# Cross attention on one Trainium2 core: the context keys' product moved behind the pair's other value products, and a wider transposition of the context probabilities

## The chip, the cores and the metric

The kernel runs on one core of a Trainium2 chip. The metric is the device time of one execution in microseconds (us). Three executions of the kernel before took 1844.14, 1845.26 and 1848.06 us; the median is 1845.26. One more execution was profiled. Engines are named as in the profile: PE is the matrix engine (PEld its weight loads), DVE the vector engine, ACT the scalar engine, POOL the general engine, SP the one that issues most DMAs.

## The reference, cut to what matters

The program is a two-layer decoder: four batches of 512 tokens with 128 features, and a context of 32 tokens per batch. Six blocks follow one another, each with a residual and a layer norm. The change is in the second block of layer 0, an attention over the 512 tokens and the 32 context tokens together:

```python
x = layer_norm(image_embeds, ln1_g, ln1_b)   # the 32 context tokens
l = layer_norm(latents, ln2_g, ln2_b)        # the 512 tokens
q = l @ Wq                                    # 16 heads of 64
kv = jnp.concatenate([x, l], axis=1) @ Wkv    # 544 keys and values
w = jnp.einsum('bhqd,bhkd->bhqk', q * scale, k * scale)
w = jax.nn.softmax(w, axis=-1)
out = jnp.einsum('bhqk,bhkd->bhqd', w, v)
return out.transpose(0, 2, 1, 3).reshape(B, S_lat, INNER) @ Wo
```

The third block, the next attention (16 heads of 8), begins inside the end of this one.

## The kernel before, in words

Everything is float32 here. Heads are taken in pairs: a *pair of heads* g (32 of them: four batches times eight) fills both halves of the array's 128 columns or rows. Each pair of heads has four *steps*, one for each 128 queries, so the stage is a loop of 128 steps i, which each engine's program walks through in its own order (`b2_pe`, `b2_act`, `b2_dve`; seven more rounds on PE and DVE drain it). The position of a step in its group of four is r = i % 4. There is no scheduler: the order is as the code writes it, and engines meet by semaphores.

In round i:

- PE computes the **scores** of step i (`scores`, L639: four matmuls of 64 rows, two at a time on the two row halves, into banks 0 to 3 of PSUM). They wait until ACT has done both exponentials of step i-1, since there is one set of banks.
- DVE takes two maxima (`neg_max`, L826), ACT two exponentials (L777), DVE then divides by the sums one round later (`normalise`, L832 and L834).
- PE **transposes** the probabilities of step i-2 (`transposes`, L653: eight of 128x128 for the 512 tokens' keys; L658: one for the 64 columns with both heads' context keys, into the rows 0 to 63 of bank 6). ACT copies the eight out (L785); DVE copies bank 6 out once for the four steps of a pair of heads (`ctx_read`, L857).
- PE multiplies the transposed probabilities with the values (`pv`, L675). This product of a pair of heads has five parts k, each with one matmul for each head, the two side by side in column halves: k = 0 to 3 are the 512 tokens (128 rows, 64 columns each), k = 4 is the context (32 rows, 64 columns each). All five add up in bank 7. Parts 0 and 1 stand at r = 3, parts 2 and 3 at r = 0, part 4 at r = 1, right behind the scores. So part 4 of the pair of heads g is in round i = 4g + 9.
- The sum is read out of bank 7 by DVE (`pv_read`, L851) in the same round, behind the two maxima of step i in DVE's order.

Bank 7 is shared. Besides the sum of the five parts it takes the projections of the next queries and keys (L596), of the next values (L628), matmuls of the norms (L623, L612), and the output projection (L684). Each of these waits for the semaphore `bank7_read`, that is for the reader of the use before. At r = 1 the use of bank 7 stands behind the transpositions, and the reading it waits for is `pv_read`.

A record of a matmul in the profile is one of two passes: a float32 matmul has two (x8 for four matmuls), a float32 transposition one.

The head of the third block runs inside the last rounds: its scores are L1112, their maxima L1390, on POOL L1337 to L1345 split its queries and keys, SP writes the rows of ones (L1520) and packs them by DMA.

Of the kernel before, what the change touches and what calls it, by code (L numbers as in the profile page):

```python
# [21 lines left out]
B, T, D = 4, 512, 128  # L22
H, HD = 16, 8
XH, XD = 16, 64
S = 32
# [49 lines left out]
def program(nc, xT, ctxT, vecs, groups, out, stages=6):  # L75
    ctx = ExitStack()
    with ctx:
# [5 lines left out]
        def sem(name):  # L83
            if name not in sem_of:
                sem_of[name] = ctx.enter_context(nc.semaphore(name))
            return sem_of[name]
# [26 lines left out]
        ps = ctx.enter_context(nc.psum_tensor("ps", [128, 8, 512], F32))  # L113
# [185 lines left out]
        P = TAPS // 2  # L299
# [146 lines left out]
        if stages >= 2:  # L446
            Wq, Wkv, Wo = wt["Wq"], wt["Wkv"], wt["Wo"]
            XP, XPAIRS, XHALF = B * 8, B * 32, KEYS // 2
# [3 lines left out]
            x_prob = c(6 * KEYS).rearrange("p (s k) -> p s k", s=3)  # L452
# [15 lines left out]
            def prob_of(P, r):  # L468
                return x_prob[:, P % 3, KEYS * r:KEYS * r + KEYS]
# [43 lines left out]
            for i in range(XPAIRS + 7):  # L513
                r, n = i % 4, i // 4 + 1
# [70 lines left out]
            def b2_pe(e):  # L585
                def free7(use):
                    if at7[use] > 1:
                        e.wait_ge(sem("bank7_read"), at7[use] - 1)
# [36 lines left out]
                def v_proj(b, j, bank):  # L625
                    k, a = divmod(j, 2)
                    e.wait_ge(*latents(b))
                    e.matmul(ps[:, bank, :], x_aux[:, b, k * 128:k * 128 + 128], Wkv[:, 1024 + a * 512:1536 + a * 512],  # L628
                             start=True, stop=True).then_inc(sem("v_proj"), 1)
# [14 lines left out]
                def transposes(P):  # L644
                    n, q = divmod(P, 4)
                    if P == 0:
                        e.wait_ge(sem("v_read"), 8)
                    for r in range(2):
                        e.wait_ge(sem("prob_done"), 2 * P + r + 1)
                        if P:  # L650
                            e.wait_ge(sem("evacuated"), 2 * P + r - 1)
                        for k in range(4):
                            i = e.transpose(ps[:, 4 + r, k * 128:k * 128 + 128], prob_of(P, r)[:, MAIN[r] + k * 128:MAIN[r] + k * 128 + 128],  # L653
                                            ident)
                        i.then_inc(sem("transposed"), 1)
                    if q == 0 and n:
                        e.wait_ge(sem("ctx_probs"), n)
                    e.transpose(ps[0:2 * S, 6, q * 128:q * 128 + 128], x_prob[:, P % 3, T:T + 2 * S],  # L658
                                ident).then_inc(sem("ctx_turned"), 1)

                def pv(g, parts):
                    b, hp = divmod(g, 8)
                    if parts[0] == 0:
                        e.wait_ge(sem("evacuated"), 8 * (g + 1))
                        if b == 0:
                            e.wait_ge(sem("v_read"), 8)
                        free7(("pv", g))
                    for k in parts:
                        if k == 4:
                            e.wait_ge(sem("ctx_probs"), g + 1)  # L670
                        for j in range(2):
                            h = 2 * hp + j
                            v_of = x_vv[:, b % 2, k, :] if k < 4 else x_vc[S * j:S * j + S, b, :]
                            p_of = x_pt[:, 2 * g % 4 + j, k, :] if k < 4 else x_ptc[S * j:S * j + S, g % 2, :]
                            i = e.matmul(ps[64 * j:64 * j + 64, 7, :], v_of[:, h * 64:h * 64 + 64], p_of,  # L675
                                         start=(k == 0), stop=(k == 4), skip_group_check=True)
                    if parts[-1] == 4:
                        i.then_inc(sem("pv_done"), 1)
# [13 lines left out]
                for i in range(XPAIRS + 7):  # L692
                    r, n = i % 4, i // 4 + 1
                    if i < XPAIRS:
                        scores(i)
                    if i < 2:
                        for j in range(4 * i, 4 * i + 4):
                            if j >= 3:
                                e.wait_ge(sem("v_read"), j - 2)
                            v_proj(0, j, 4 + j % 3)  # L700
                    if r == 1:
                        if 0 <= (i - 9) // 4 < XP:
                            pv((i - 9) // 4, (4,))
                    if i == XPAIRS + 5:
                        head_pe(e, range(*HEAD[i]))
                    if i == XPAIRS + 6:
                        head_pe(e, range(HEAD[i][0], HEAD[i][0] + 3))
                    if r == 2:
                        if out_at(i - 1) is not None:
                            out(out_at(i - 1), 1)  # L710
                        elif n < XP:
                            proj("q", n)
                    if r == 3:
                        if v_at(i):
                            free7(("v",) + v_at(i))
                            v_proj(*v_at(i), 7)
                        elif early_at(i):
                            early(early_at(i))
                        elif chain_at(i):
                            chain(chain_at(i))  # L720
                        if late(i) and n < XP:
                            proj("k", n)
                    if 0 <= i - 2 < XPAIRS:
                        transposes(i - 2)
                    if r == 3 and 0 <= (i - 7) // 4 < XP:
                        pv((i - 7) // 4, (0, 1))
                    if r == 0 and 0 <= (i - 8) // 4 < XP:
                        pv((i - 8) // 4, (2, 3))
                    if r == 1:
                        if out_at(i) is not None:  # L730
                            out(out_at(i), 0)
                        elif v_at(i):
                            free7(("v",) + v_at(i))
                            v_proj(*v_at(i), 7)
                        elif early_at(i):
                            early(early_at(i))
                        elif chain_at(i):
                            chain(chain_at(i))
                    if r == 2 and n < XP:
                        proj("q" if late(i) else "k", n)  # L740
                    if i in HEAD_QK:
                        head_qk_pe(e, HEAD_QK[i])
                    if i in HEAD and i != XPAIRS + 5:
                        head_pe(e, range(HEAD[i][0] + (3 if i == XPAIRS + 6 else 0), HEAD[i][1]))
# [229 lines left out]
        def narrow(nth, src, src_ready, dst, tag, load, wq, wk, wv, wo, bias_v=None, rope=None, early=None, head=0, border=None):  # L974
# [82 lines left out]
            for step in range(STEPS):  # L1057
                G, u = step // 16, step % 16
                g, r = raw_group(step)
# [436 lines left out]
            def sp(e):  # L1496
                for b in range(B):
                    for i, ready in ((0, 1), (1, 3), (2, 4)):
                        for w in range(2):
                            e.wait_ge((split_q, split_k)[w], 4 * b + ready)  # L1500
                            for r in ((i, i + 3) if w and i < 2 else (i,)):
                                e.dma_start(scr[b, w, 8 * r:8 * r + 8].rearrange("d (h t) -> (d h) t", h=H),
                                            (parts if b else parts_0)[:, w, i, :]).then_inc(parts_out, 16)
                    e.wait_ge(parts_out, 16 * 8 * (b + 1))
                    if early is not None and b < 2:
                        e.wait_ge(sem("pv_done"), (24, XP)[b])
                    for hg in range(4):
                        if b:
                            e.wait_ge(packed[hg], 16 * 6 * (batches_0 + b))
                        if b >= 2:  # L1510
                            e.wait_ge(score2, 64 * (b - 2) + 16 * (hg + 1))
                        for w in range(2):
                            pack(e, b, w, hg)
                    if b == 0:
                        e.wait_ge(ones_set, nth + 1)
                        for a in range(2):
                            if a and early is not None:
                                e.wait_ge(sem("pv_done"), XP)
                            for hg in range(4):
                                e.dma_start(k_pack[a][hg][ROWS:ROWS + 3, :, :],  # L1520
                                            ones_row.unsqueeze(1).to_broadcast([3, 4, T])).then_inc(ones_rows, 16)
# [1399 lines left out]
```

## Time and profile before

| | us |
|---|---|
| median of three executions | 1845.26 |
| the profiled execution | 1845.25 |
| its span, first to last instruction | 1843.4 |
| PE busy in the span | 1653.6 (90%) |
| DVE busy | 1271.4 (69%) |
| ACT busy | 949.4 (52%) |
| scores of step 0 to the last context product | about 60 to 674 |

The profiled execution lies at the median. The span leaves 1.85 us around it. Times in the rows are us from the span's start. The clock that was granted to PE is given as a share of full speed (2.4 GHz). Share of busy time says little about what a change is worth: PE's share in the stage in question is high, and what has to be read is which wait ends last before each piece.

### The profile page before, as it was taken

Reading aid. Unit: us, or ns where it says so; the run is one execution under the profiler, and the core shown is the slowest. Engines: PE = TensorE matmul, PEld = TensorE weight load, DVE = VectorE, ACT = ScalarE, POOL = GpSimd, SP = SyncE. Lnnn points to the kernel's source line nnn. Section 1 sums busy time; section 2 is a strip of 40 time slices with the busy share of each in tenths; the row PEclk is TensorE's granted clock in tenths of the full one; section 3 lists DMA queues with packets and bytes.
Section 4 is the critical chain, followed back from the end, with each engine's and each line's share of the span. In section 5 each row is a group of like instructions: output and inputs, shape, how many; then the busy total and the mean of one; then the engine's idle time right before and its main releaser. Section 6 shows DMA issues by size and latency. Waiting matters only on the chain.

```text
span 1843.4 us, 24921 instructions
## 1 busy us (share of the span) xinstructions
PE 1653.6 (90%) x8074; PEld 736.0 (40%) x8074; DVE 1271.4 (69%) x2994; ACT 949.4 (52%) x2053; POOL 304.5 (17%) x465
## 2 busy tenths in 40 slices
PE   7899999999999989999899988444798899999998
PEld 3355455545544432222244331222443355444443
DVE  7576666767667768888565578999666677762423
ACT  3565556556645516666633566333236366664333
POOL 1000000000001021121277200000000222114443
PEclk9999999999999989999999999777799799999999
DMA  4000000000000220240000000000100512100000
GB/s 193 1 1 1 1 1 1 1 1 1 1 1 21 55 59 23 73 116 2 1 0 1 0 1 1 1 1 1 69 1 1 147 55 73 32 2 1 1 0 23
DMA packets 19806, 44.36 MB, mean 24 GB/s; under 512 B 3872, under 2 KB 13024, under 8 KB 18912
## 3 DMA queue, kind: packets, MB, share of 16 engines
q1 hardware_dynamic: 19200, 42.39, 7.6%
q8 instruction: 66, 1.08, 0.2%
q14 instruction: 60, 0.49, 0.1%
q10 hardware_dynamic: 480, 0.39, 0.1%
HBM read 32.74 MB, written 9.44 MB: 23 GB/s over the span
## 4 chain that ended last, share of the span: by engine, by line
PE 75%; DVE 16%; ACT 5%; issue 3%; POOL 1%; DMA 0%; ACTq 0%; POOLq 0%; SPq 0%; DVEq 0%
PE ps L675 8%; PE ps L639 8%; PE ps L653 6%; PE ps L1226 6%; PE ps L1264 5%; PE ps L1112 5%; PE ps L1699 3%; PE ps L1700 3%; PE ps L596 3%; PE ps L1596 3%; PE ps L1612 3%; PE ps L1707 3%; DVE arena L2063 2%; PE ps L684 2%; DVE arena L2050 2%
## 5 line engine op out<-in xcount | busy, mean ns | idle before, releaser
L1390 DVE TENSOR_REDUCE stat<-ps 128x1 f32<-128x512 f32 (+3 forms) x512 | 279.1, 581 | 86.6 <-PE ps L1116 43.0
L1321 ACT ACTIVATE arena<-ps 128x512 f32<-128x512 f32 (+3 forms) x512 | 247.1, 515 | 154.3 <-PE ps L1264 83.3
L826 DVE TENSOR_REDUCE stat<-ps 128x1 f32<-128x544 f32 x256 | 173.4, 719 | 163.0 <-PE ps L639 163.0
L777 ACT ACTIVATE arena<-ps,stat 128x544 f32<-128x544 f32 x256 | 180.7, 711 | 201.9 <-DVE stat L826 201.9
L1264 PE MATMUL ps<-arena 75*128 75x512 bf16 (+1 forms) x480 | 163.1, 344 | 11.7 <-ACT arena L1321 9.5
L1112 PE MATMUL ps<-arena 72*128 72x128 bf16 (+1 forms) x480 | 163.0, 348 | 8.0 <-DVE stat L1390 7.8
L675 PE MATMUL ps<-arena 128*64 128x512 f32 (+1 forms) x640 | 159.2, 609 | 4.7 <-DVE arena L845 3.3
L639 PE MATMUL ps<-arena 64*128 64x272 f32 x1024 | 152.1, 415 | 5.1 <-ACT arena L777 4.3
L785 ACT COPY arena<-ps 128x512 f32<-128x512 f32 x256 | 137.3, 594 | 15.5 <-PE ps L653 15.5
L653 PEld LDWEIGHTS ps<-wA_sb,arena 128*128 128x128 f32 x1024 | 115.1, 142 | 70.1 <-issue 68.9
L653 PE MATMUL ps<-wA_sb,arena 128*128 128x128 f32 x1024 | 138.3, 278 | 0.0
L639 PEld LDWEIGHTS ps<-arena 64*128 64x128 f32 x1024 | 88.2, 186 | 113.0 <-ACT arena L777 67.6
L1730 DVE TENSOR_TENSOR arena<-arena,ps 128x512 f32<-128x512 f32 (+1 forms) x76 | 52.2, 687 | 116.6 <-ACT arena L1719 116.5
L834 DVE TENSOR_SCALAR arena<-arena,stat 128x544 f32<-128x544 f32 x256 | 120.1, 511 | 4.5
L1949 ACT ACTIVATE reg<-arena,reg 128x16 f32<-128x16 f32 x254 | 66.3, 315 | 103.3 <-DVE arena L2063 103.3
L1226 PE MATMUL ps<-arena 128*32 128x512 f32 (+3 forms) x1024 | 116.2, 527 | 0.0
L958 POOL COPY arena<-arena 64x32 f32<-64x32 f32 x64 | 15.4, 240 | 582.1 <-PE ps L639 548.2
L1719 ACT ACTIVATE arena<-ps 128x512 f32<-128x512 f32 (+1 forms) x76 | 45.3, 597 | 127.5 <-PE ps L1700 127.5
L2163 PE MATMUL ps<-reg 128*128 128x512 f32 (+1 forms) x120 | 66.7, 674 | 41.0 <-DVE reg L2095 33.2
L1744 POOL TENSOR_TENSOR arena<-arena 128x512 f32<-128x512 f32 x64 | 82.7, 1292 | 95.4 <-DVE arena L1730 95.4
L1112 PEld LDWEIGHTS ps<-arena 72*128 72x128 bf16 x480 | 47.3, 99 | 116.8 <-DVE stat L1390 65.1
L1632 POOL TENSOR_TENSOR reg<-reg,arena 128x512 f32<-128x512 f32 x64 | 88.7, 1404 | 24.5 <-ACT reg L1622 23.6
(391 smaller groups left out, 2775.2 us busy)
## 6 DMA issues: line engine op xcount, KB each, us to landing
arena<-b_parts SPq DMA_DIRECT2D x180, 96.0 KB
b_parts<-arena SPq DMA_DIRECT2D x64, 128.0 KB, 1.9
reg<-wM_dram SPq DMA_DIRECT2D x1, 3072.0 KB, 10.0
reg<-wB_dram SPq DMA_DIRECT2D x1, 2048.0 KB, 12.4
reg<-wM_dram SPq DMA_DIRECT2D x1, 2048.0 KB, 16.7
reg<-wD_dram SPq DMA_DIRECT2D x1, 1817.0 KB, 10.7
wF_sb<-wF_dram SPq DMA_DIRECT2D x1, 1476.0 KB, 19.8
reg<-b_parts SPq DMA_DIRECT2D x12, 96.0 KB
```

Source lines behind the costliest of these rows:

```text
L639: i = e.matmul(ps[:, 2 * r + a, 0:XHALF], x_qq[64 * r:64 * r + 64, n % 2, q * 128:q * 128 + 128], x_kt[64 * r:64 * r + 64, n % 2, S * (1 - ...
L653: i = e.transpose(ps[:, 4 + r, k * 128:k * 128 + 128], prob_of(P, r)[:, MAIN[r] + k * 128:MAIN[r] + k * 128 + 128], ident)
L675: i = e.matmul(ps[64 * j:64 * j + 64, 7, :], v_of[:, h * 64:h * 64 + 64], p_of, start=(k == 0), stop=(k == 4), skip_group_check=True)
L777: e.activation(prob_of(P, r).rearrange("p (a k) -> p a k", a=2), score_banks(r), ACT.Exp, bias=x_neg[:, at_:at_ + 1], accum_out=x_sums[:, ...
L785: e.copy(x_pt[:, 2 * n % 4 + r, :, q * 128:q * 128 + 128], ps[:, 4 + r, :].rearrange("p (k q) -> p k q", k=4)).then_inc(sem("evacuated"), 1)
L826: e.tensor_reduce(x_neg[:, n % 4:n % 4 + 1], score_banks(r), AX.XY, ALU.max, negate=True).then_inc(sem("max_done"), 1)
L834: e.tensor_scalar(prob_of(P, r), prob_of(P, r), x_inv[:, at_ + r:at_ + r + 1], None, ALU.mult).then_inc(sem("prob_done"), 1)
L1112: i = e.matmul(ps[:, step % S1, 0:keys(u)], q_pack[pack][hg][0:ROWS, h, q * 128:q * 128 + 128], k_pack[pack][hg][0:ROWS, h, 0:keys(u)], st ...
L1226: i = e.matmul(ps[32 * j:32 * j + 32, 5, q0:T], vv[:, b % 2, p, G % 4 * 4 + j, :], p_t[:, n_ % 2 * 4 + j, q0:T], start=(p == 0), stop=(p = ...
L1264: i = e.matmul(ps[:, S1 + m % S2, q0:T], k_pack[pack][hg][0:ROWS + 3, h, k * 128:k * 128 + 128], q_pack[pack][hg][0:ROWS + 3, h, q0:T], st ...
L1321: e.activation(p_t[:, m % 8, q0:T], ps[:, S1 + m % S2, q0:T], ACT.Exp).then_inc(exp_done, 1)
L1390: e.tensor_reduce(nm[:, G % 2, u // 4, u % 4:u % 4 + 1], ps[:, step % S1, 0:keys(u)], AX.X, ALU.max, negate=True).then_inc(max_done, 1)
```

## The change

Three edits. The context product (part 4) moves from r = 1, behind the scores, to r = 0, behind parts 2 and 3. The transposition of the context probabilities takes 128 columns (the 64 context columns and 64 more that nobody reads) in place of 64. And SP waits for the split of the second batch before it writes the second set of rows of ones.

```diff
@@ transposes
-                    e.transpose(ps[0:2 * S, 6, q * 128:q * 128 + 128], x_prob[:, P % 3, T:T + 2 * S],
+                    e.transpose(ps[:, 6, q * 128:q * 128 + 128], x_prob[:, P % 3, T:T + 128],
                                 ident).then_inc(sem("ctx_turned"), 1)
@@ the loop of b2_pe
                             v_proj(0, j, 4 + j % 3)
-                    if r == 1:
-                        if 0 <= (i - 9) // 4 < XP:
-                            pv((i - 9) // 4, (4,))
                     if i == XPAIRS + 5:
...
                     if r == 0 and 0 <= (i - 8) // 4 < XP:
                         pv((i - 8) // 4, (2, 3))
+                        pv((i - 8) // 4, (4,))
@@ sp, the rows of ones
                             if a and early is not None:
                                 e.wait_ge(sem("pv_done"), XP)
+                                e.wait_ge(split_q, 8)
+                                e.wait_ge(split_k, 8)
```

PE's order from a transposition at r = 0 to the use of bank 7 at r = 1, before. L675 64x512 is the value product, L639 the scores, L653 and L658 the transpositions, L628 a projection of values:

```order
L658 MATMUL ps<-wA_sb,arena 64x128
L675 MATMUL ps<-arena 64x512 x4
L639 MATMUL ps<-arena 128x272 [waits ctx_keys,bank7_read,exp_done]
L639 MATMUL ps<-arena 128x272 x3
L675 MATMUL ps<-arena 64x512 [waits ctx_probs]
L675 MATMUL ps<-arena 64x512
L653 MATMUL ps<-wA_sb,arena 128x128 [waits evacuated,prob_done]
L658 MATMUL ps<-wA_sb,arena 64x128
L628 MATMUL ps<-reg,x_aux 128x512 [waits c_normed,bank7_read]
```

The same place after the change:

```order
L658 MATMUL ps<-wA_sb,arena 128x128
L675 MATMUL ps<-arena 64x512 x4
L675 MATMUL ps<-arena 64x512 [waits ctx_probs]
L675 MATMUL ps<-arena 64x512
L639 MATMUL ps<-arena 128x272 [waits ctx_keys,bank7_read,exp_done]
L639 MATMUL ps<-arena 128x272 x3
L653 MATMUL ps<-wA_sb,arena 128x128 [waits evacuated,prob_done]
L658 MATMUL ps<-wA_sb,arena 128x128
L628 MATMUL ps<-reg,x_aux 128x512 [waits c_normed,bank7_read]
```

The two matmuls of part 4 now stand ahead of the scores of r = 1. DVE's order at r = 1 after the change (the line numbers are two lower than before; L824 the maxima, L849 `pv_read`, L855 `ctx_read`):

```order
L824 TENSOR_REDUCE stat<-ps 128x1 [waits exp_done,scored] x2
L849 COPY cent<-ps 128x512 [waits pv_done]
L830 RECIPROCAL stat<-stat 128x2 [waits exp_done]
L832 TENSOR_SCALAR arena<-arena,stat 128x544 [waits dve_link]
L832 TENSOR_SCALAR arena<-arena,stat 128x544
L855 COPY arena<-ps 64x512 [waits pv_done,ctx_turned]
```

Nothing moved there: the reading of bank 7 still stands behind the two maxima, which wait for the scores of the same round.

## Rows read from the trace of the kernel before

**Rows 1.** The page, part 1: busy time, share and instructions of each engine.
```profile
PE 1653.6 (90%) x8074; PEld 736.0 (40%) x8074; DVE 1271.4 (69%) x2994; ACT 949.4 (52%) x2053; POOL 304.5 (17%) x465
```

**Rows 2.** Windows: stretch, length, busy time of PE, PEld, DVE, ACT, POOL, clock, DMA.
```profile
409.15:413.27 4.12, 4.12 (x27) 2.11 (x26) 2.34 (x5) 2.14 (x6) 0.00 (x0) 1.00 0.00 0
413.27:417.55 4.28, 4.28 (x25) 2.12 (x24) 3.03 (x7) 2.63 (x7) 0.00 (x0) 1.00 0.00 0
```

**Rows 3.** Chain that ended last, from 411 us: start, us, what.
```profile
411.47 1.87 PE ps L675 x8
413.34 1.12 PE ps L639 x8
414.46 1.00 PE ps L675 x4
415.46 1.02 PE ps L653 x8
416.49 0.11 PE ps L658
...
421.97 1.12 PE ps L639 x8
```

**Rows 4.** Timeline, 411 to 417 us: start, us, engine, line, op, [idle before <-releaser].
```profile
411.88 0.14 PEld L675 LDWEIGHTS ps<-arena 128*64 128x64 f32 x2 [0.29 <-issue]
...
412.31 0.14 PEld L675 LDWEIGHTS ps<-arena 128*64 128x64 f32 x2 [0.29 <-issue]
...
413.27 1.19 PE L639 MATMUL ps<-arena 64*128 64x272 f32 x8
...
414.49 1.36 DVE L826 TENSOR_REDUCE stat<-ps 128x1 f32<-128x544 f32 x2 [1.74 <-PE ps L639]
...
415.76 0.68 DVE L851 COPY cent<-ps 128x512 f32<-128x512 f32 x1
...
416.49 0.30 PEld L623 LDWEIGHTS ps<-reg,wA_sb 128*128 128x128 f32 x2 [0.17 <-DVE cent L851]
```

**Rows 5.** Line L851 (`pv_read`): who waited for it, us and times.
```profile
  PEld ps L628: 2.0, 12
  PEld ps L623: 1.4, 8
  PEld ps L612: 1.0, 6
  PEld ps L684: 0.5, 3
```

**Rows 6.** Timeline of the one r = 1 without a use of bank 7, from 501.20 us.
```profile
501.20 1.19 PE L639 MATMUL ps<-arena 64*128 64x272 f32 x8
...
504.73 1.19 PE L639 MATMUL ps<-arena 64*128 64x272 f32 x8 [0.21 <-ACT arena L777]
```

**Rows 7.** Timeline, 655 us: a context transposition, then the next block's scores.
```profile
655.20 0.27 PE L658 MATMUL ps<-wA_sb,arena 128*64 128x128 f32 x1
...
655.31 0.81 PE L1112 MATMUL ps<-arena 72*128 72x512 bf16 x3
```

**Rows 8.** Chain that ended last, 668 to 676 us: the end of the stage.
```profile
668.98 2.22 POOL arena L1345 x2
...
672.42 0.39 PE ps L1131 x4
672.81 1.03 PE ps L675 x4
673.86 0.69 DVE dev L851
```

**Rows 9.** Timeline, 652 to 674 us: DVE and SP at the end of the stage.
```profile
652.94 1.89 DVE L1390 TENSOR_REDUCE stat<-ps 128x1 f32<-128x512 f32 x3 [2.33 <-PE ps L1112]
...
670.15 3.08 DVE L1390 TENSOR_REDUCE stat<-ps 128x1 f32<-128x512 f32 x5 [2.01 <-PE ps L1112]
...
673.86 2.94 SPq L1520 DMA_DIRECT2D arena<-arena  x4
```

## The prediction

> **What bounds the kernel now.** I read part 1 of the page first: PE is busy 90% of the span, so every place where PE is the last to be ready costs time, and every place where it waits hides some [rows 1]. Then the windows of single rounds of the attention. A round at r = 0 lasts 4.12 us and one at r = 1 lasts 4.28 us, both at the full clock [rows 2]. From the starts of the scores (L639) I took the lengths of all rounds: they repeat to 0.01 us, so one place read closely stands for some thirty.
>
> The chain that ended last lies on PE alone at r = 0 and r = 1: parts 2 and 3 of the value product 1.87 us, scores 1.12, part 4 (L675 x4) 1.00, eight transpositions 1.02, the context transposition 0.11 [rows 3]. Read without the next view, this says that the order of these pieces is free, and only their sum counts. The timeline says otherwise. At r = 1 the scores start at 413.27. DVE is idle for 1.74 us, waiting for them, and takes both maxima from 414.49 on. Only behind these stands the reading of bank 7, at 415.76 for 0.68 us, to 416.44. PE's next use of bank 7 starts at 416.49, and its releaser is this reading [rows 4]. So the use starts 416.49 - 413.27 = 3.22 us behind the scores. PE itself comes to it after 1.12 + 1.00 + 1.02 + 0.11 = 3.25 us by the chain's lengths, or, by the recorded 0.17 us of idle time less the 0.11 us of L658, about 0.06 us before the reading is done. Two paths of equal length thus end there: PE's (scores, part 4, transpositions) and DVE's (scores, maxima, reading). DVE's does not hold part 4 unless part 4 ends later than the maxima, and it does not.
>
> How often: the reading's waiters are 12 + 8 + 6 + 3 = 29 uses of bank 7 [rows 5]. There are 30 rounds at r = 1 with a part 4 inside the 128 steps; the thirtieth has no use of bank 7.
>
> **The change part by part.**
>
> Part 4 at r = 0. It comes behind parts 2 and 3 and ahead of the scores of r = 1, which wait for nothing but PE's own end there (4.12 us a round against 3.53 us where the exponentials bound it [rows 2, 6]). So the round at r = 0 grows by all that part 4 costs. Its price in the old place is 1.00 us [rows 3]. It is two passes' time and a switch: the pairs of weight loads of parts 2 and 3 follow at 412.31 - 411.88 = 0.43 us, so two pairs stream for 0.86 us, and 0.14 us are left for what comes with a change of shape. The new place is bounded from both sides: 0.86 us if the step from 128 rows and 64 columns to 32 rows and 64 columns costs nothing, 1.00 us if it costs what the step out of 32 rows costs now. No row shows this step. The nearest is the step from the scores, 64 rows and 128 columns, to the transpositions, 128 rows and 128 columns: there too only the rows change, and the scores take 1.12 us as they do ahead of part 4, where rows and columns change (the piece at 421.97 against that at 413.34) [rows 3]. I take 1.00.
>
> The Trainium skill, "TensorEngine Tiling (Array Packing)", Key Properties, says "Mode switching requires drain", for a change of the tiling mode and not just of the tile. The trace agrees with it in the 1.12 us just named. By this rule the step costs its switch, and the sum stays at 1.00 a piece.
>
> Part 4 taken out of r = 1. PE then has scores 1.12 and transpositions 1.02 + 0.11 = 2.25 us, and reaches the use of bank 7 one microsecond sooner. DVE's path stays as it is, since its order has the reading behind the two maxima of that round and they wait for its scores. That bank 7 is complete a round earlier does not help: DVE stands in its queue at the first maximum, which is the 1.74 us of idle time [rows 4], and now stands there about 2.7 us. The use still starts 3.22 us behind the scores, with about 1.0 us of idle PE ahead of it. The round stays at 4.28 us, and nothing is taken back. Behind the waiting matmul in PE's queue stand the scores of r = 2, and the maxima and exponentials that wait for them.
>
> The thirtieth round at r = 1 has no such use. It lasts 504.73 - 501.20 = 3.53 us, and the scores that end it wait for ACT's exponential [rows 6]; scores, maxima and exponentials have the same lengths after. It stays too.
>
> So 30 rounds at r = 0 grow by 1.00 us: +30.0 us. Rounds at r = 2 and 3 have no edit but the transposition.
>
> The transposition at 128 columns. Its weight load grows from 64 to 128 columns, and lies beside the transposition before it. Its own step on PE is 0.11 us now, with the wide ones' eight at 1.02 less their 0.14 of entry, so 0.11 each [rows 3]: the step is set by the 128 moving columns, which stay. If the cover failed, a step of 0.11 would be added at each of 128 places, 14 us; the wide ones stand against it, since they step by 0.11 with that very load. A gain could come if the narrow one cost a switch: but after a narrow one the next block's 128-column scores follow at 655.31 - 655.20 = 0.11 us [rows 7], no switch at all. I take zero; the bounds are -0.09 and +0.11 for each, and the upper one is the less likely, since the same load is seen hidden eight times in each round.
>
> The Trainium skill, "TensorEngine Tiling (Array Packing)", Restrictions, says that column tiling disables the transpose mode for float32. By that the narrow transposition cannot have been column-tiled, and the wide one removes no switch; the trace agrees in the same 0.11 us.
>
> SP's new waits. The second rows of ones were issued at 673.86, released by the last part 4 [rows 9]. The split of the second batch ends at 668.98 + 2.22 = 671.20, ahead of it [rows 8]. After the change the last part 4 comes earlier against its surroundings and the split's end is what is late, but ahead of the old time. Queued behind on SP are the parts and packs of the second batch, which come no later than before. Cost zero. Without that cover, the wait would push four issues (2.94 us [rows 9]) and what is queued behind them back by as much as the split ends late.
>
> The end of the stage. The pair of heads 30 has part 4 at 653, between the next block's first three scores and transpositions. DVE had been idle 2.33 us waiting for those three [rows 9], and from there its maxima pace the chain. Part 4 now stands ahead of them: +1.00 us. The last pair has its part 4 at 672.81, behind the POOL chain's turn at 672.42, and DVE reads it at 673.86 [rows 8]. DVE's five maxima from 670.15 end at 673.23, so it idled 0.63 us for part 4. With part 4 ahead of the five, they start 1.00 later (DVE was idle for PE there, 2.01 us) and the 0.63 goes: +0.37 us.
>
> Sum: 30.0 + 1.0 + 0.4 = +31.4 us. All that follows hangs rigidly on the end of this stage. The profiled execution took 1845.25 us (span 1843.4, 1.85 around it), the median of the runs is 1845.26, so no correction: 1876.6 us.
>
> **The rivals.**
>
> No switch between parts 3 and 4. For it: both are 64 columns wide. Against it: the 1.12 us at 421.97. Each of 32 pieces is 0.14 shorter: 31.4 - 32 x 0.14 = +26.9, 1872.2 us.
>
> The wide transposition saves a drain behind it after all. For it: parts 2 and 3, which follow such a transposition, take 1.87 us where four pairs stream for 4 x 0.43 = 1.72, so 0.15 goes at their two ends [rows 3, 4]. Against it: the step of 0.11 in [rows 7], and the products are column halves, so a switch stays behind a full-width piece. At 0.09 in each of 128: 31.4 - 11.5 = +19.9, 1865.2 us.
>
> The clock falls. PE gets a new idle microsecond in 29 rounds. Against it: the windows at r = 0 and 1 have 1.00, as has the stretch with the exponential wait. If in each of 30 groups of four rounds 0.33 us of work ran at half speed, 30 x 0.33 = 10 us are added: 1886 us.
>
> The other side: it is not slower. The mechanism would be that the switch around part 4 is saved while the use of bank 7 does not wait for DVE at r = 1, because the reading is done in DVE's idle 1.74 us ahead of the maxima. Then PE goes on at 2.25 us. It decides as soon as the reading ends by 2.25 us behind the scores' start, and where the exponentials (3.53 us a round) are not next. PE would save the one switch between the scores and part 4, or pay none: 32 x -0.14 = -4.5, 1840.8 us. If the exponentials are next, r = 0 and 1 together are 5.12 + 3.53 = 8.65 against 8.40, +0.25 x 30 = +7.5, 1852.8 us. Against both: DVE's order is unchanged, and each of the 29 uses has DVE as its releaser now [rows 5].
>
> **How the numbers follow.** Forecast (1876.6, its own scatter 1874 to 1879) 0.68. No switch 0.17. A cheaper transposition 0.04. Clock 0.05. Not slower 0.03, the exponentials' version 0.03. The range goes from 1870.5, below the no-switch case, to 1879.5; what is left out is 0.15. No change from change can be told in this kernel at about 0.2%, 3.7 us. Slower by more: 0.68 + 0.17 + 0.04 + 0.05 + 0.03 = 0.97, less a little for what I have not seen, 0.95; within 0.2%: 0.03; faster: 0.02.
>
> **What would show it.** Right: rounds at r = 0 of 5.12 us, at r = 1 still 4.28 us with about 1.0 us of idle PE ahead of L628, L623, L612 and L684 put down to the reading of bank 7; the wait of DVE for the scores at 2.7 us; L675 x12 in 2.87 us from the start of part 2 to the scores; L658 at steps of 0.11. Rounds at r = 0 of 4.98 show the no-switch rival. A reading of bank 7 ahead of the maxima, or a round at r = 1 under 4.2 us, shows the forecast wrong in its main step. Clock under 1.00 in rounds of the first three batches shows the clock's.

## The result, and the profile after

The changed kernel takes 1876.47 us, the median of six executions, against 1844.70 for the six of the kernel before. The ratio is 1.0171, with a 95% interval of 1.0148 to 1.0194: slower, by about 31.5 us. One of the six executions took 2420.70 us in a disturbed state; without it the median is 1875.12, and the ratio is made without it. The forecast was 1876.6.

The profiled execution of the changed kernel took 1874.14 us, 28.9 more than that of before. First the page after, part 1, with busy time, share and instructions of each engine. It answers to [rows 1].

```profile
PE 1654.5 (88%) x8069; PEld 738.1 (39%) x8074; DVE 1271.4 (68%) x2994; ACT 948.4 (51%) x2053; POOL 304.4 (16%) x465
```

The engines work hardly more than before: PE 0.9 us, its weight loads 2.1 us, the others nothing. Nearly all of the 28.9 us is idle time of PE. The same two rounds as in [rows 2], with the stretch, its length, busy time of PE, PEld, DVE, ACT and POOL, and the clock:

```profile
426.70:431.82 5.12, 5.12 (x31) 2.33 (x30) 2.34 (x5) 2.46 (x6) 0.00 (x0) 1.00 0.00 0
431.82:436.10 4.28, 3.38 (x21) 1.95 (x20) 3.03 (x7) 2.30 (x6) 0.00 (x0) 1.00 0.00 0
```

The round at r = 0 went from 4.12 to 5.12 us and is PE's alone. The round at r = 1 stayed at 4.28 us, although PE is busy for only 3.38 of it. The timeline of these rounds shows where the rest went. It answers to [rows 4]; the columns are start, us, engine, line, operation, and the idle time before it with its releaser. DVE's maxima are L824 here and the reading of bank 7 is L849.

```profile
428.75 0.27 PE L658 MATMUL ps<-wA_sb,arena 128*128 128x128 f32 x1
428.95 2.94 PE L675 MATMUL ps<-arena 128*64 128x512 f32 x12
...
430.81 0.19 PEld L675 LDWEIGHTS ps<-arena 32*64 32x64 f32 x4 [0.81 <-issue]
431.82 0.76 PEld L639 LDWEIGHTS ps<-arena 64*128 64x128 f32 x8 [0.81 <-issue]
431.82 1.19 PE L639 MATMUL ps<-arena 64*128 64x272 f32 x8
...
433.04 1.36 DVE L824 TENSOR_REDUCE stat<-ps 128x1 f32<-128x544 f32 x2 [2.74 <-PE ps L639]
...
434.31 0.68 DVE L849 COPY cent<-ps 128x512 f32<-128x512 f32 x1
...
435.05 1.12 PE L623 MATMUL ps<-reg,wA_sb 128*128 128x512 f32 x2 [0.91 <-DVE cent L849]
...
436.10 1.19 PE L639 MATMUL ps<-arena 64*128 64x272 f32 x8
```

Part 4 now lies inside the L675 x12 from 428.95. From its start to the scores are 431.82 - 428.95 = 2.87 us, 1.00 more than parts 2 and 3 took alone; from the weight loads of part 4 to the scores are 431.82 - 430.81 = 1.01 us. Bank 7 is complete when the scores of r = 1 start at 431.82, but DVE reads it only at 434.31, behind the maxima, and waits 2.74 us for their scores. PE's use of bank 7 starts 435.05 - 431.82 = 3.23 us behind the scores, as before, now with 0.91 us of idle PE ahead of it.

The line of the reading, by who waited for it (us, times), answers to [rows 5]:

```profile
  PEld ps L628: 13.7, 12
  PE ps L628: 10.9, 12
  PEld ps L623: 9.1, 8
  PE ps L623: 7.2, 8
  PEld ps L612: 6.9, 6
  PE ps L612: 5.4, 6
  PEld ps L684: 3.4, 3
  PE ps L684: 2.7, 3
```

The four lines of PE make 26.2 us of idle time in 29 places. The weight loader's own waits at the same places, 2.0 + 1.4 + 1.0 + 0.5 us in [rows 5], are 33.1 us now.

### The profile page after: what moved, and what is told of

Read it like the earlier page. It is cut to its first block, busy times and chain, and to the rows that moved or that the text cites. A ratio compares the mean times of both kernels' runs of the same rounds, so it can differ in the third digit from the quotient of the medians.

```text
span 1872.3 us, 24917 instructions
## 1 busy us (share of the span) xinstructions
PE 1654.5 (88%) x8069; PEld 738.1 (39%) x8074; DVE 1271.4 (68%) x2994; ACT 948.4 (51%) x2053; POOL 304.4 (16%) x465
## 4 chain that ended last, share of the span: by engine, by line
PE 72%; DVE 18%; ACT 5%; issue 4%; DMA 0%; POOL 0%; ACTq 0%; POOLq 0%; SPq 0%; DVEq 0%
PE ps L675 8%; PE ps L639 8%; PE ps L1224 5%; PE ps L1262 5%; PE ps L1110 5%; PE ps L653 4%; PE ps L1699 3%; PE ps L1700 3%; PE ps L596 3%; PE ps L1596 3%; PE ps L1707 3%; PE ps L1612 3%; DVE arena L2063 2%; DVE stat L824 2%; PE ps L628 2%
## 5 line engine op out<-in xcount | busy, mean ns | idle before, releaser
L824 DVE TENSOR_REDUCE stat<-ps 128x1 f32<-128x544 f32 x256 | 173.5, 719 | 192.9 <-PE ps L639 192.9
L675 PE MATMUL ps<-arena 128*64 128x512 f32 (+1 forms) x640 | 157.8, 612 | 4.7 <-DVE arena L843 3.4
L639 PE MATMUL ps<-arena 64*128 64x272 f32 x1024 | 152.0, 415 | 6.1 <-ACT arena L775 5.3
L653 PE MATMUL ps<-wA_sb,arena 128*128 128x128 f32 x1024 | 136.8, 277 | 0.0
L653 PEld LDWEIGHTS ps<-wA_sb,arena 128*128 128x128 f32 x1024 | 114.0, 141 | 55.3 <-issue 53.9
L639 PEld LDWEIGHTS ps<-arena 64*128 64x128 f32 x1024 | 88.1, 186 | 113.0 <-issue 58.2
```

What stands on the lines that cost most here:

```text
L639: i = e.matmul(ps[:, 2 * r + a, 0:XHALF], x_qq[64 * r:64 * r + 64, n % 2, q * 128:q * 128 + 128], x_kt[64 * r:64 * r + 64, n % 2, S * (1 - ...
L824: e.tensor_reduce(x_neg[:, n % 4:n % 4 + 1], score_banks(r), AX.XY, ALU.max, negate=True).then_inc(sem("max_done"), 1)
```

## The experiments

In the first four, the kernels ran on one chip beside 25 executions of the kernel before (median 1844.96 us), in the last three beside seven (median 1845.15). The ratios are those on record and not quotients of these medians (for part 4 done twice, which ran from 1865.71 to 1885.34 us, that would be 1.0120). The lengths of rounds are differences between the starts of the scores (L639) in each trace.

### The move alone

```diff
-                    e.transpose(ps[:, 6, q * 128:q * 128 + 128], x_prob[:, P % 3, T:T + 128],
+                    e.transpose(ps[0:2 * S, 6, q * 128:q * 128 + 128], x_prob[:, P % 3, T:T + 2 * S],
```

> The changed kernel with the context transposition back at 64 columns; the move and SP's waits stay. If the move is the whole cost, this runs like the changed kernel: 1875 us, rounds at r = 0 of 5.12 us and at r = 1 of 4.28. If the wide transposition saved or cost a switch of 0.09 us at each of 128 places, it is 11 us away from it.

Measured: 1875.23 us, ratio 1.0147 (1.0084 to 1.0211). The rounds at r = 0 last 5.12 us and those at r = 1 4.28, as in the changed kernel. The move is the whole cost, together with SP's waits, which are in this kernel too.

### The wide transposition alone

```diff
-                    e.transpose(ps[0:2 * S, 6, q * 128:q * 128 + 128], x_prob[:, P % 3, T:T + 2 * S],
+                    e.transpose(ps[:, 6, q * 128:q * 128 + 128], x_prob[:, P % 3, T:T + 128],
```

> The kernel before with the wide context transposition alone. If the step is set by the 128 moving columns: 1845 us and L658 at steps of 0.11. If the wider weight load shows: up to +14 us. If a switch goes: down to -11 us.

Measured: 1846.24 us, ratio 0.9999 (0.9974 to 1.0024). The rounds are those of the kernel before, 4.12 and 4.28. The line L658 by engine, operation, count and duration (ns, least, median, most) in this kernel:

```profile
L658 PEld LDWEIGHTS ps<-wA_sb,arena x128: 139/141/231, 72.8 to 656.0; 128*128 128x128 f32 x128
L658 PE MATMUL ps<-wA_sb,arena x128: 272/273/421, 72.9 to 656.1; 128*128 128x128 f32 x128
```

The weight load is recorded with a median of 141 ns in place of 111, the matmul with 273 ns, as before. The added 30 ns lie beside the transposition ahead of it. Neither the gain nor the loss in the bounds of this term is there.

### Part 4 left out

```diff
-                    if r == 1:
-                        if 0 <= (i - 9) // 4 < XP:
-                            pv((i - 9) // 4, (4,))
...
-                                         start=(k == 0), stop=(k == 4), skip_group_check=True)
-                    if parts[-1] == 4:
+                                         start=(k == 0), stop=(k == 3), skip_group_check=True)
+                    if parts[-1] == 3:
```

SP's two waits are in this kernel too.

> The kernel before with part 4, the context's product, left out (the output lacks the context's values); pv_done is raised by part 3. PE has 32 x 1.00 us less to do. If the use of bank 7 at r = 1 is held by DVE's reading behind the maxima, part 4 was hidden at r = 1 and only the end of the stage gains: 1844 us, r = 1 still 4.28. If PE's sum bounds r = 1: 1813 us. If the exponentials take over at once: r = 1 at 3.53, 1823 us.

Measured: 1846.00 us, ratio 1.0012 (0.9981 to 1.0044). PE has 32 us less to do and the kernel is no faster. Its two rounds, as windows:

```profile
410.48:414.59 4.11, 4.11 (x27) 2.10 (x25) 2.34 (x5) 2.14 (x6) 0.00 (x0) 1.00 0.01 4
414.59:418.88 4.29, 3.38 (x22) 1.93 (x20) 3.03 (x7) 2.64 (x7) 0.00 (x0) 1.00 0.00 0
```

The second has the length and PE's 3.38 us of the changed kernel's round at r = 1. In the kernel before, part 4 stood in time that PE would have waited for DVE anyway. This is the experiment that tells the two readings of the chain apart: by the chain alone each part 4 was 1.00 us of bound work [rows 3], and taking it out gives nothing.

### Part 4 done twice in the old place

```diff
+                            pv((i - 9) // 4, (5,))
                             pv((i - 9) // 4, (4,))
...
-                        if k == 4:
+                        if k >= 4:
                             e.wait_ge(sem("ctx_probs"), g + 1)
```

> The kernel before with part 4 done twice at r = 1 (the context's values are counted twice). If PE's path and DVE's path to the use of bank 7 are of one length, PE's takes over at once: rounds at r = 1 grow by 0.86 less the 0.06 of wait there is, to 5.07, and the time by 29 x 0.80 + 0.6 + 0.9 = 24.7 us, to 1869.5. If DVE's reading had slack to give beyond that 0.06, less.

Measured: 1867.33 us, ratio 1.0147 (1.0097 to 1.0196). A round at r = 1 lasts 4.97 us, 0.69 more and not the 0.80 expected. PE's timeline of one:

```profile
423.41 1.19 PE L639 MATMUL ps<-arena 64*128 64x272 f32 x8
424.52 1.93 PE L675 MATMUL ps<-arena 32*64 32x512 f32 x8
426.39 1.09 PE L653 MATMUL ps<-wA_sb,arena 128*128 128x128 f32 x8
427.32 0.27 PE L658 MATMUL ps<-wA_sb,arena 128*64 128x128 f32 x1
427.43 1.02 PE L623 MATMUL ps<-reg,wA_sb 128*128 128x512 f32 x2
428.38 0.50 PE L639 MATMUL ps<-arena 64*128 64x272 f32 x2
```

L623 follows L658 after 0.11 us and the scores follow it after 428.38 - 427.43 = 0.95 us. Its weight load starts at 427.32, with the transposition. In the kernel before, where L623 had waited for DVE, the scores followed after 417.55 - 416.50 = 1.05, and its weight load started with it, at 416.49 [rows 4]. So the use that waited had its weight load in the open, and this one has it under the transposition. So the wait of 0.06 us cost 0.06 + 0.10 = 0.17 us (4.28 + 0.86 - 4.97), and that was the whole difference between the two paths in the kernel before. With nothing in part 4's place DVE's path binds, with two there PE's does.

### The reading ahead of the maxima

```diff
+                    if r == 1 and 0 <= (i - 9) // 4 < XP:
+                        pv_read((i - 9) // 4)
                     if i < XPAIRS:
                         neg_max(i, 0)
                         neg_max(i, 1)
-                    if r == 1 and 0 <= (i - 9) // 4 < XP:
-                        pv_read((i - 9) // 4)
```

> The changed kernel with DVE's reading of bank 7 moved ahead of the two maxima of the same round. If this reading holds PE: r = 1 falls from 4.28 to 3.53, where the exponentials bound it (26 rounds), and the three rounds with the output projection by 0.97: -22.4 us, 1853 us, still about 8 over the kernel before. If PE alone then bounds r = 1 (3.30): 1848. If the reading does not hold PE: 1875, as the changed kernel.

Measured: 1861.06 us, ratio 1.0073 (1.0045 to 1.0101). That is some 14 us under the changed kernel, where 22 were expected. The timeline shows the mechanism as expected at r = 1, and what takes the rest at r = 2:

```profile
421.34 1.19 PE L639 MATMUL ps<-arena 64*128 64x272 f32 x8
421.46 0.69 DVE L849 COPY cent<-ps 128x512 f32<-128x512 f32 x1 [1.64 <-PE ps L675]
...
423.50 1.02 PE L623 MATMUL ps<-reg,wA_sb 128*128 128x512 f32 x2
...
424.88 1.19 PE L639 MATMUL ps<-arena 64*128 64x272 f32 x8 [0.35 <-ACT arena L775]
425.66 0.72 ACT L788 ACTIVATE reg<-ps,vec 128x512 f32<-128x512 f32 x1
...
426.52 1.10 PE L596 MATMUL ps<-x_aux,reg 128*128 128x512 f32 x2 [0.46 <-ACT reg L788]
```

DVE reads bank 7 right behind part 4, at 421.46. The use starts 423.50 - 421.34 = 2.16 us behind the scores with no wait, and the round ends at 3.54 us by the exponentials. This settles the cause. But r = 2 grows from 4.34 to 4.54 or 4.64 us: PE's projection of queries (L596) needs bank 7 again, and now waits for ACT, which reads the use at r = 1 only behind its exponentials and copies. The resource is the same bank, its next reader is another engine. In the profiled executions the stretch from the first to the last scores is 599.3 us against 612.8 in the changed kernel: -23.0 at r = 1 (26 x 0.75 + 3 x 1.17), +4.8 at r = 2 in the first three batches, and +5 in the last batch, where the granted clock also differs (0.96 against 1.00 over its last 95 us). Of these 5 us, 4.2 are three rounds at r = 2 of 7.68, 7.92 and 7.62 us against 6.32, 6.38 and 6.32; the kernel before has such long rounds too, with PE at half the clock in them (see the next section). The rest is 0.3 us each in two more rounds at r = 2, as above, and 0.2 in two others.

### One shape for all five parts

```diff
-                            v_of = x_vv[:, b % 2, k, :] if k < 4 else x_vc[S * j:S * j + S, b, :]
-                            p_of = x_pt[:, 2 * g % 4 + j, k, :] if k < 4 else x_ptc[S * j:S * j + S, g % 2, :]
+                            v_of = x_vv[:, b % 2, min(k, 3), :]
+                            p_of = x_pt[:, 2 * g % 4 + j, min(k, 3), :]
```

> The changed kernel with part 4's two matmuls on part 3's operands, 128 rows in place of 32, so all five parts have one shape (the output lacks the context's values and counts one part twice). If the step from 128 to 32 rows costs a switch: rounds at r = 0 of 4.98 in place of 5.12, 32 x 0.14 = 4.4 us less than the changed kernel, about 1871. If it costs nothing: no difference in these rounds, 5.12.

Measured: 1870.98 us, ratio 1.0143 (1.0124 to 1.0162). A round at r = 0, as a window, and the one behind it:

```profile
423.60:428.57 4.97, 4.97 (x31) 2.42 (x29) 2.34 (x5) 2.46 (x6) 0.00 (x0) 1.00 0.00 0
428.57:432.86 4.29, 3.38 (x22) 1.96 (x20) 3.03 (x7) 2.31 (x6) 0.00 (x0) 1.00 0.00 0
```

4.97 or 4.98 in all thirty, 0.14 us under 5.12. Four times the rows cost no time, and the change of rows alone, with the columns unchanged, costs a switch (the 0.14 us that come with a change of shape, beside the 0.86 us of streaming).

### The changed kernel once more

> The changed kernel once more, beside the others, for a second profile. Rounds at r = 0 of 5.12 and at r = 1 of 4.28 in every repetition, and the differences between executions only in rounds that have a granted clock under 1.00: 1876 us.

Measured: 1874.63 us, ratio 1.0175 (1.0147 to 1.0202). All rounds have the lengths of the first profile, to 0.01 us. The two profiled executions still differ by 2.0 us (spans of 1872.3 and 1870.3), and 1.94 of it lies ahead of the first scores (60.18 against 58.24), where the clock is 0.94 in both from 30 us on. So the expectation that executions differ only by their clock was too narrow.

## Why the prediction was right

Its steps in turn, between the two profiled executions.

**Part 4 at r = 0: +30.0.** Measured 30 rounds of 5.12 against 4.12, +30.0. The bound taken (1.00 with a switch, and not 0.86) was right, and the run with one shape shows the 0.14 directly.

**Nothing taken back at r = 1.** Of the 29 rounds with a use of bank 7, 26 measured 4.28 us and the three with the output projection 6.86, all as before; the one without a use measured 3.53, as before. Part 4 left out, and the reading moved, show that DVE's place for the reading held PE; the second of them removes the wait.

**The paths at r = 1 as of equal length.** Right in kind. The 0.06 us was undersized as a price: the wait also lays the next weight load open, 0.10 us more. It did not enter the sum, since it is there before and after. The 3.25 us added up for PE's path were too long, since the chain cuts its pieces at their ends: L658 at 416.32 and its step of 0.11 give 416.32 + 0.11 - 413.27 = 3.16 us. With 0.86 us more in front of it, in the kernel with part 4 done twice, it is 427.43 - 423.41 = 4.02.

**The transposition: 0, SP's waits: 0.** The first is shown by its own run. The second rows of ones were issued at 701.78, which is 28.8 us behind the last scores (672.96), against 28.5 before (673.86 - 645.39). The forecast had them ahead of the old time; they come 0.3 us behind it, since they now wait for the split, which ends at 701.69, 28.7 us behind the last scores. What follows on SP had no waiter on the critical chain. SP's waits alone were not taken out of the changed kernel, since a race would be open; the kernel without part 4 has them and is not slower.

**The end of the stage: +1.4.** Undersized. The chain that ended last, after the change, in this end:

```profile
688.55 0.70 DVE stat L1388
...
689.91 3.57 PE ps L675 x8
...
700.59 3.08 DVE stat L1388 x5
703.67 0.60 DVE dev L849
...
705.53 5.91 PE ps L684 x8
```

The same pieces in the kernel before, from its chain:

```profile
659.99 0.70 DVE stat L1390
...
661.13 1.87 PE ps L675 x8
...
675.82 6.28 PE ps L684 x8
```

Counted from the last scores (645.39 before, 672.96 after), the maximum at 688.55 comes 15.59 us behind them against 14.60: +1.0 for the part 4 of the pair of heads 30, as forecast. Then parts 0 and 1 of the last pair take 3.57 us against 1.87, at a granted clock of 0.52. DVE's five maxima follow, and the reading stands behind them with no idle time of its own, as forecast: 673.86 - 645.39 = 28.47 us before and 703.67 - 672.96 = 30.71 after, +2.2 and not +1.4. The five maxima start 2.87 us later (27.63 against 24.76 us behind the last scores) and not 2.0. The excess of 0.87 us is the half clock's. It was there before too, but on parts 2 and 3 of the same pair, as the timelines show, before and after:

```profile
666.80 2.77 PE L675 MATMUL ps<-arena 128*64 128x512 f32 x8
```

```profile
697.28 2.94 PE L675 MATMUL ps<-arena 128*64 128x512 f32 x12
```

Parts 2 and 3 take 1.94 us in this view at the full clock, so 0.83 us were lost there before and none after, when the x12 has part 4 in it too. On parts 0 and 1 it costs 1.70 us now, and the difference is 0.87. The output projection gives 0.4 back (5.91 against 6.28), so the end costs +1.8.

**What the sum did not have.** In the profiled executions the stretch from the first scores to the last grew by 27.1 us and not by 30. The last 13 rounds before the last scores hold three of the grown ones, and last 64.2 us in both. The windows of these, before and after:

```profile
581.20:645.39 64.19, 57.49 (x304) 30.35 (x304) 45.90 (x85) 34.24 (x82) 8.21 (x12) 0.95 0.19 54
```

```profile
608.80:672.96 64.16, 54.75 (x305) 28.82 (x304) 45.92 (x85) 34.01 (x82) 8.21 (x12) 1.00 0.20 54
```

The granted clock was 0.95 before and 1.00 after. Three rounds hold the difference: 7.75, 7.86 and 5.38 us before, 6.38, 6.32 and 5.25 after, 3.0 us together. In this stretch PE waits some 2 us for DVE, and in the kernel before it then runs at half speed for a while:

```profile
584.57 1.10 PE L596 MATMUL ps<-x_aux,reg 128*128 128x512 f32 x2 [2.19 <-DVE reg L904]
...
585.51 1.58 PE L653 MATMUL ps<-wA_sb,arena 128*128 128x128 f32 x8
```

Eight transpositions take 1.58 us here against 1.04 in the same view one round later, at 591.15, and the granted clock from 584.57 to 588.94 is 0.64. The changed kernel has the wait too, and kept the full clock in both of its profiles. So 3 us of the 31 were given back by the clock in these executions. It is no sure gain: of such long rounds at r = 2 the kernel with the wide transposition alone has three, the one with the reading ahead three, the one without part 4 one and the one with part 4 twice one, while the move alone and the kernel with one shape have none. Why the clock falls in some and not in others is open. The whole is then +0.4 ahead of the first scores (less than the 1.94 by which the two profiles of the changed kernel differ there), +27.1 in the rounds (30.0 less the clock's 3), +1.8 at the end of the stage and -0.5 behind it: 28.8 of the 28.9. The clock rival, a fall because of the new idle microsecond, did not come: the rounds with it have 1.00.

The runs differ by more than the profiled pair: the medians of five executions after and six before by 30.4 us, the means behind the ratio by 31.5, the medians of the repetition by 29.5. The forecast's 31.4 is at the upper end of these. The mechanism was right, and so was the price of the 30 pieces. That the total of 1876.6 met 1876.47 to 0.1 us is luck: the median of the five is 1875.12, 1.5 us lower, and in the profiled pair 0.4 too little at the end of the stage stood against 3 too much for the clock.

## What to carry to other kernels

A chain that ended last on one engine does not say that this engine's sum is the bound: here two paths of nearly one length met at the shared bank, and the chain showed only one of them. Before moving work on one engine, read which wait stands right behind its old place and by how much it was hidden; here 1.00 us of work filled a wait of nearly 1.00 us, so taking it out gave nothing and putting it elsewhere cost its full length. A result that is ready sooner helps only if its reader's queue reaches it sooner, and here moving one reader ahead uncovered the next reader of the same bank.

## What the hardware showed beyond this

Going from value products of 128 rows to ones of 32 with the same 64 columns costs 0.14 us, as much as part 4 paid in its old place behind the scores, where rows and columns change; 128 rows in place of 32 cost nothing. A matmul of 512 columns that had waited for a semaphore took 1.05 us to the next piece, and 0.95 where it had not waited and its weight load lay under the transposition before it. A transposition with 64 columns behind ones of 128 has no switch ahead of it: its step is 0.11 us, and the rounds are 4.12 and 4.28 us with 64 or 128 columns of weights. The granted clock in a stretch with the same waits was 0.95 in one kernel and 1.00 in the other, worth 3 us in 64.
